# Ternary feed-forward inside the frequency attention, two batches behind it, and the first feed-forward's weights prepared in the first attention

## The reference

```python
# layer 0 feed-forward: bit-linear, depthwise convolution, silu, bit-linear
def weight_quant(w):
    scale = 1.0 / jnp.clip(jnp.mean(jnp.abs(w)), 1e-05)
    return jnp.clip(jnp.round(w * scale), -1, 1) / scale
def act_quant(x):                      # per position
    scale = 127.0 / jnp.clip(jnp.max(jnp.abs(x), axis=-1, keepdims=True), 1e-05)
    return jnp.clip(jnp.round(x * scale), -128, 127) / scale
# h = bit_linear(layernorm(x), w1); h = silu(conv3(h)); x += g * bit_linear(h, w2)
# w1 is 1024 x 256, w2 is 256 x 1024

# layer 1 attention (per batch): layernorm, rfft over the positions, 16 heads of
# attention of the 513 frequencies to those of the context, irfft, x += g * (y @ Wo.T)

# layer 1 feed-forward
delta = 0.7 * jnp.mean(jnp.abs(w))     # w is 256 x 256
wt = jnp.where(w > delta, 1.0, jnp.where(w < -delta, -1.0, 0.0))
# x += g * (alpha * layernorm(x) @ wt.T + bias)
```

## Time and profile before

| | |
|---|---|
| median of the runs | 1948.39 us (3 runs) |
| the profiled execution's own time | 1948.08 us |
| its span | 1946.1 us |
| TensorE busy | 1656.8 us (85% of the span) |
| DVE busy | 1148.0 us (59%) |
| ACT busy | 886.7 us (46%) |
| `l0x` from its first operation to its last | until 179.29 us |
| `l0f`, first operation to first `up` product | 180.67 to 213.58 us |
| `l1x` | 475.85 to 751.70 us |
| `l1f` | 752.93 to 806.24 us |

### The profile page before, as it was taken

One profiled execution on the slowest core, in us unless ns is written; L12 is line 12 of the kernel. 1 busy time (PEld: TensorE's weight loads), 2 busy tenths in 40 slices (PEclk: granted clock), 3 DMA queues, 4 the chain that ended last, 5 costly groups with the idle time before them and its releaser, 6 DMA issues. The chain is left out here.

```text
span 1946.1 us, 29978 instructions
## 1 busy us (share of the span) xinstructions
PE 1656.8 (85%) x10149; PEld 1254.6 (64%) x10149; DVE 1148.0 (59%) x2495; ACT 886.7 (46%) x1803; POOL 321.2 (17%) x359
## 2 busy tenths in 40 slices
PE   7895578896899997899997579999954999979998
PEld 5452245555677665588886269999944888854446
DVE  4765567676455556899887743322247889842115
ACT  2232567764443210365564345555544566533213
POOL 0000000000000001311100155555553111101110
PEclk9898799998899988999998779999977999979999
DMA  5001000002100000100001922222252000010002
GB/s 154 1 1 44 0 1 1 1 1 68 49 1 1 1 1 9 30 1 1 2 2 55 382 82 72 72 72 72 72 168 67 2 1 2 1 47 1 1 0 87
DMA packets 62845, 78.78 MB, mean 40 GB/s; under 512 B 13179, under 2 KB 52655, under 8 KB 62319
## 3 DMA queue, kind: packets, MB, share of 16 engines
q1 hardware_dynamic: 42967, 47.35, 7.4%
q0 software_dynamic: 7584, 20.72, 3.4%
q10 hardware_dynamic: 12152, 8.85, 1.5%
HBM read 58.16 MB, written 18.74 MB: 40 GB/s over the span
## 5 line engine op out<-in xcount | busy, mean ns | idle before, releaser
L2880 PEld LDWEIGHTS moe_bank<-moe_xt,moe_w1e 128*128 128x128 f32 x1264 | 155.0, 193 | 5.7 <-DVE moe_xt L2728 1.7
L2880 PE MATMUL moe_bank<-moe_xt,moe_w1e 128*128 128x128 f32 x1264 | 155.8, 277 | 1.1 <-DVE moe_xt L2728 1.1
L2890 PE MATMUL moe_bank<-moe_w,moe_xin 128*128 x632 | 149.3, 379 | 0.0
L2954 ACT ACTIVATE moe_xin<-moe_bank,moe_b 128x128 f32<-128x128 f32 x316 | 90.1, 368 | 125.8 <-PE moe_bank L2880 124.2
L390 PE MATMUL l0f_hb<-l0f_xt,l0f_w 128*128 128x512 f32 x256 | 126.0, 624 | 5.4 <-DVE l0f_a L321 3.8
L1092 POOL TENSOR_TENSOR all_x<-all_x,l1f_bias 128x256 f32 x32 | 23.1, 724 | 632.2 <-DVE l1f_xn L204 632.2
L2890 PEld LDWEIGHTS moe_bank<-moe_w,moe_xin 128*128 128x128 f32 x632 | 114.0, 190 | 12.3
L209 DVE BATCH_NORM_STATS2 all_stats<-all_x 128x6 f32<-128x256 f32 (+1 forms) x256 | 104.0, 422 | 8.4
L2737 DVE TENSOR_TENSOR moe_y<-moe_bank,moe_b2r 128x256 f32<-128x256 f32 x79 | 33.6, 425 | 119.0 <-PE moe_bank L2890 116.1
L2797 POOL DMA_INDIRECT moe_results<-moe_y,moe_row x79 | 78.0, 987 | 125.1 <-DVE moe_y L2737 121.1
L2728 DVE COPY moe_xt<-moe_bank 128x256 f32<-128x256 f32 x79 | 33.6, 425 | 106.2 <-PE moe_bank L2868 105.1
(11 more groups left out here) (478 smaller groups left out, 3812.1 us busy)
## 6 DMA issues: line engine op xcount, KB each, us to landing
moe_w<-in_L_ffn_W SPq DMA_DIRECT2D x32, 512.0 KB, 10.3
moe_w<-moe_results SPq DMA_DIRECT2D x16, 512.0 KB, 8.8
all_x<-in_x SPq DMA_DIRECT2D x4, 1024.0 KB, 13.1
out_x<-all_x SPq DMA_DIRECT2D x8, 512.0 KB, 2.9
l0f_w<-in_L_ffn_w_T SPq DMA_DIRECT2D x2, 1024.0 KB, 6.4
moe_inputs<-moe_xin ACTq DMA_DIRECT2D x8, 256.0 KB, 7.3
moe_inputs<-moe_w1e ACTq DMA_DIRECT2D x8, 256.0 KB, 7.5
moe_b2r<-in_L_ffn_b SPq DMA_DIRECT2D x1, 2048.0 KB, 14.0
```

The source lines that it names most:

```text
L2880: ins = nc.tensor.matmul(out, w1e[:, at:at + P], xt[:, u, c * P:(c + 1) * P], start=(c == 0), stop=(c == DC - 1))
L2890: ins = nc.tensor.matmul(bank[4 + u][:, 0:D], ht[:, u, c * P:(c + 1) * P], w2[:, ds(e * (HC * D) + c * D, D)], start=(c == 0), stop=(c == ...
L2954: ins = nc.scalar.activation(ht[:, u, m * P:(m + 1) * P], bank[1 + u][:, m * P:(m + 1) * P], ACT.Gelu, bias=b1[:, ds(e * HC + m, 1)])
```

## The change

1. A scope `f0` (w1, w2, scales, eight normalised tiles) lives over `l0x` and `l0f`. SP fetches `w1` and `w2` in `l0x`, behind the loads of `x`. In `l0x` ACT takes the two absolute sums at the end of round b=0, TensorE adds them over the partitions in round b=1, DVE makes the scales and rounds `w1` at the ends of rounds b=1 and b=2, and in round b=3 it computes the norm of the first eight tiles (`norm_range`), normalises them and makes their scales. `l0f` then starts with the eight quantising passes on ACT; the silu table and the scaling of `w2` come behind the first copies, the norm of the other 24 tiles behind the eight dequantising passes.
2. The stage `l1f` is gone. Its weights are fetched in `l1x`; DVE sums and rounds them in rounds b=0 and b=1. In rounds b=2 and b=3 the eight tiles of batch b-2 pass through the feed-forward in between the attention's work. Each takes one of the three `gbank` banks from its turn to its update, so `ORDER` gets 32 more names. Between a batch's last `update` and the `offset` of the next batch's query stands `next_norm` (the norm scale and shift of that batch, 19 small DVE operations). Behind the loop come the inverse and output of batch 3 with the feed-forward of batch 2 in between, then `next_norm(3)` and the feed-forward of batch 3 alone.
3. In rounds 1 to 3, `output(6)` of batch b-1 comes behind `scores(b, 4)` and ahead of `dft(b+1, 2)`; before it stood ahead of `values(b, 3)`.

```diff
 # l0x, ACT, end of round b
+                    if b == 0:
+                        act.wait_ge(sh.f0_loaded, 32)
+                        nc.scalar.activation(f.w2q[:, :, :].rearrange("p m d -> p (m d)"), f.w1[:, :, :].rearrange("p m d -> p (m d)"), ACT.Abs,
+                                             accum_out=f.wsum[:, 0:1]).then_inc(sh.f0_wsum, 1)
...
 # l0x, DVE, in round b
+                    else:
+                        dve.wait_ge(s.xn_ready, T)
+                        dve.wait_ge(s.stats_ready, 2 * TB)
+                        norm_range(nc, c, sh, 0, TB)
                     if b:
                         update(b - 1, 2)
                     if b + 1 < B:
                         norm(b + 1, NP, TB)
+                    else:
+                        next_inputs()
                     if b:
                         update(b - 1, 3)
+                        if b == 1:
+                            weight_scales()
+                        elif b == 2:
+                            round_weights()
+                        else:
+                            next_scales()
...
 # l0f, ACT
                 for t in range(TB):
-                    norm(t)
-                for t in range(TB):
                     quantise_x(t)
                 for t in range(0, TB, 2):
                     copy_x(t)
...
 # l1x, ORDER of rounds 1 to 3
+            ORDER += some("q2", b, 0, 4) + (some("sum", 0, 0) if b == 1 else ffn(0))
+            ORDER += some("it", b - 1, 0, 2) + ffn(1) + some("it", b - 1, 2, 4) + ffn(2)
+            ORDER += (some("dft", b + 1, 0, 2) if new else []) + ffn(3)
+            ORDER += some("out", b - 1, 0, 2) + ffn(4) + some("out", b - 1, 2, 5) + ffn(5) + some("out", b - 1, 5, 7) + ffn(6)
+            ORDER += (some("dft", b + 1, 2) if new else []) + some("out", b - 1, 7) + ffn(7)
...
 # l1x, DVE
+                def ffn_update(e, j):
+                    n = e * TB + j
+                    dve.wait_ge(s.fy_ps, n + 1)
+                    dve.wait_ge(s.f_biased, n + 1)
+                    nc.vector.tensor_tensor(x_tile(sh, n), gb("ffn", e, j)[:, D:2 * D], x_tile(sh, n), ALU.add).then_inc(s.fx_ready, 1)
...
                     if old:
                         update(b - 1, 6)
+                    if fed:
+                        ffn_update(e, 6)
+                    if old:
                         update(b - 1, 7)
+                    if fed:
+                        ffn_update(e, 7)
+                    if old:
+                        next_norm(b - 1)
+                    else:
+                        weight_sums()
                     if new:
                         offset(b + 1, 0)
                         offset(b + 1, 1)
...
 # l1x, PE
+                def ffn_turn(e, j):
+                    n = e * TB + j
+                    bank = free("ffn", e, j)
+                    pe.wait_ge(s.fxn_ready, n + 1)
```

More of the change, by code:

```diff
@@ L568, in stage_l0_xattn @@
     s = scope(nc, "l0x")
+    f = sh.f0
+    HID = 4 * D
     SC = D ** -0.5
@@ L1013, in _ @@
                         base(3)
+                    if b == 1:
+                        pe.wait_ge(sh.f0_wsum, 2)
+                        pe.wait_ge(s.shared_set, 1)
+                        nc.tensor.matmul(ub[:, 0:2], sh.ones[:, :], f.wsum[:, :], start=True, stop=True).then_inc(sh.f0_wtot, 1)
                     if b + 1 < B:
@@ L1246, in stage_l1_xattn @@
+        ORDER += some("it", B - 1, 0, 2) + some("ffn", B - 2, 0) + some("it", B - 1, 2, 4) + some("ffn", B - 2, 1)
+        for j in range(0, TB, 2):
+            ORDER += some("out", B - 1, j, j + 2) + some("ffn", B - 2, 2 + j // 2)
+        ORDER += some("ffn", B - 2, 6, 8) + some("ffn", B - 1, 0, 8)
         PLACE = {g: i for i, g in enumerate(ORDER)}
@@ L1397, in _, with weight_sums @@
                 offset(0, 1)
[L1398 to L1410 removed]
+                def weight_sums():
+                    dve.wait_ge(s.f_loaded, 48)
+                    nc.vector.tensor_reduce(fsum[:, :], fw[:, :, :], AX.XY, ALU.add, apply_absolute_value=True).then_inc(s.fsum_ready, 1)
@@ new lines, in _ @@
+                for b in range(B):
+                    old, new, e = b > 0, b + 1 < B, b - 2
+                    fed = e >= 0
+                    if old:
+                        result(b - 1, 4)
+                    if fed:
+                        ffn_norm(e, 0)
+                        ffn_norm(e, 1)
+                    shift(b, 0)
+                    if new:
+                        fold_halves(b + 1)
+                    sums(b, 0)
+                    if fed:
+                        ffn_update(e, 0)
+                    if b == 1:
+                        ternary_weights()
+                    result(b, 0)
+                    shift(b, 1)
@@ L1604, in _, with weight_total @@
                 pe.wait_ge(s.kbd_ready, 4)
-                for b in range(B + 1):
-                    live, old, new = b < B, b > 0, b + 1 < B
-                    if live:
-                        scores(b, 0)
-                        if b == 0:
-                            turn_values(0)
-                        for i in range(4):
-                            query(b, 1, i)
-                        turn(b, 0)
+                def weight_total():
+                    pe.wait_ge(s.fsum_ready, 1)
+                    nc.tensor.matmul(free("sum", 0, 0)[:, 0:1], sh.ones[:, :], fsum[:, :], start=True, stop=True).then_inc(s.fsum_ps, 1)
@@ L1614, in _ @@
+                for b in range(B):
+                    old, new, e = b > 0, b + 1 < B, b - 2
+                    fed = e >= 0
+                    scores(b, 0)
+                    if b == 0:
+                        turn_values(0)
+                    for i in range(4):
+                        query(b, 1, i)
+                    if b == 1:
+                        weight_total()
+                    if fed:
+                        ffn_turn(e, 0)
+                    turn(b, 0)
                     if old:
@@ L1636, in _ @@
+                    turn(b, 2)
                     if b == 0:
@@ L1673, in _ @@
                         dft(b + 1, 3)
+                    if fed:
+                        ffn_product(e, 7)
+                    if old and new:
                         dft(b + 1, 4)
                         dft(b + 1, 5)
-                    if live:
-                        values(b, 4)
+                    values(b, 4)
                     if new:
@@ L1680, in _ @@
                             query(b + 1, 0, i)
+                b, e = B - 1, B - 2
+                inverse(b, 0)
+                inverse(b, 1)
+                ffn_turn(e, 0)
+                inverse(b, 2)
+                ffn_product(e, 0)
+                inverse(b, 3)
+                ffn_turn(e, 1)
+                for j in range(0, TB, 2):
+                    output(b, j)
+                    ffn_product(e, 1 + j // 2)
+                    output(b, j + 1)
+                    ffn_turn(e, 2 + j // 2)
+                ffn_product(e, 5)
+                ffn_turn(e, 6)
+                ffn_product(e, 6)
+                ffn_turn(e, 7)
+                ffn_product(e, 7)
+                ffn_turn(b, 0)
+                for j in range(TB):
+                    if j + 1 < TB:
+                        ffn_turn(b, j + 1)
+                    ffn_product(b, j)
             @block.scalar
@@ L1809, in _ @@
                             copy_q(b + 1, 0, i)
+                for e in (B - 2, B - 1):
+                    for j in range(TB):
+                        ffn_copy(e, j)
 def stage_l3_ffn(nc, io, sh, out):
```

494 lines of the change are left out of this document (266 added, 228 removed).

## The result

The changed kernel takes 1918.31 us, the median of four runs (1916.69 to 1921.12), against 1948.36 us for the kernel before in the same comparison: a ratio of 0.985, 95% interval 0.9833 to 0.9867. The forecast was 1924, its range 1908 to 1945. The profiled execution took 1919.29 us, with a span of 1917.6.

The account below looks back on a forecast made before the run. The prediction took preparation waits to bound the start of `l0f`, and TensorE the loop of `l1x`. 1948.1 - 16.2 (part 1) - 8.5 (part 2) = 1923.4 us, 1923.7 against the median, stated as 1924; range 1908 to 1945, the forecast's own 1917 to 1931.

Parts of the forecast that it names:

- Part 1, the new beginning of `l0f`: Start of `l0f`: quantising passes 3.3 us, then 6.3 from first copy to first `up` product; a gain of 23.2 us.
- Part 1, what it adds in `l0x`: In `l0x`: absolute sums 3.9, clock dip 2.0, ones product 0.5, norm work left over 0.65; 7.0 us added.
- one more dip: In `l0x`, TensorE's clock falls after idling about 3.5 us behind ACT's sums, so products run slowly: 2.0 us.
- Part 2, the rounds: Loop of `l1x`: rounds 1, 2 and 3 change by -1.8, +13.3 and +10.1 us, +21.6 in all.
- for the late DVE: `l1x` round 2, before the next query: 1.5 us because two updates and statistics in front make DVE late.
- Part 2, the end: Behind the loop of `l1x`: from the inverse of batch 3 onward 50.6 us instead of 80.7, a gain of 30.1.
- rival B: `l1x` loop swallows the tiles in idle times: loops +13 instead of +21.6, 1915 us, or 1911 with `l0x` catching up; chance 0.20.
- A: In `l1x`, every feed-forward turn waits for a bank, clock dips each round: about 12 us more, 1936; chance 0.30 with D.
- C: In `l1x`, one chain of three banks makes each tile pay a full wait: loops cost 57 us, 1959 total; chance 0.09.
- D: Only part 1 gains, its `l0x` delay caught up or not; part 2 nets zero: 1932 us; chance 0.30 with A.
- GpSimd beside DVE: POOL's bias adds, 0.72 us a tile beside DVE in `l1x`, cost nothing; by the port-lock rule up to 17 us.
- The case that the prediction feared: In `l1x`, 24 GpSimd adds of 0.72 us lock out DVE's sums and folds, holding DVE for up to 17 us.

Follow-up runs that it names:

- the tiles behind the loop: Against the changed kernel, all 32 feed-forward tiles put behind the loop of `l1x`, `output(6)` left behind `scores(b,4)`: 1913.81 us.
- part 2 alone: Against the kernel before, only the second layer's feed-forward put inside `l1x`, with the first layer of before: 1936.14 us, ratio 0.9953.
- three updates early: Against the changed kernel, update 4, the feed-forward's update 5 and update 5 moved on DVE ahead of `result(b,3)` in rounds 1 to 3: 1910.67 us.

## Why the prediction was right

- **Part 1, the new beginning of `l0f`: right.** Forecast 9.6 us from the stage's first operation to the first `up` product and a gain of 23.2, measured 9.4 and 23.5.
- **Part 1, what it adds in `l0x`: mis-sized.** Forecast 3.9 + 2.0 + 0.5 + 0.65 = 7.0. Measured 2.1 in the exps' stretch (six profiles), 3.7 in one and 5.1 in two, and 0.2 to 0.3 for the rest in round 3. In the changed kernel's own profile it is 5.3. The step that failed is "DVE has no other work to bring forward, so I count 3.9 in full" together with one more dip: DVE's update was late by 3.2 us, but the wait of 3.58 us that stood later in the round, and its dip, shrank in return. The second dip came in three of nine executions, in which the two products there took 1.72, 1.76 and 2.05 us. I had cited that wait as the model for the new one and did not ask what became of it.
- **Part 2, the rounds: right in detail.** Forecast -1.8, +13.3, +10.1; measured -2.1, +12.9, +9.8 (+8.1 for round 3 in the executions at 54.4). Within round 2 the starts of `scores(2, 0)`, `(2, 3)`, `(2, 4)` and `(3, 0)` give +3.6, +4.1 and +5.2 for the forecast 3.5, 4.3 and 5.5. TensorE's waits were 0.79 and 0.87 where I had taken 1.1 twice, 2.47 where I had taken the same, and 1.88 where I had taken 1.8. The further 1.5 us "for the late DVE" have no wait of their own. The sum credits the third edit in round 1 alone; the tiles behind the loop show that it was worth 2.3 and 3.4 us in rounds 2 and 3 as well, and that the tiles used this up.
- **Part 2, the end: a little too good.** Forecast 50.6 from the inverse of batch 3 to the last statistics, measured 52.3 (724.58 to 776.84). The inverses took 16.8 as forecast; outputs with batch 2 17.6 for 16.8; the norm 3.6 as forecast; batch 3 14.3 for 13.4. Each of the last three tiles of batch 2 took 1.82 us (753.37, 755.20, 757.02), with a wait of 0.47 us for ACT's copy, where I had taken 1.6; why batch 3 took longer is not shown.
- **The total: in part luck.** Between the forecast (1923.4) and the profiled time (1919.29) lie 4.1 us. The terms of the sum miss by 1.3 together: 1.7 us less were added in `l0x` and 1.0 less in the rounds, 0.3 more were gained at the beginning, and 1.7 less were gained at the end. Then 3.3 us come from `l0f` behind its first product (2.1) and from the way to `scores(0, 0)` (1.2). The sum has no term for them, and kernels with the same code in these stages also differ by as much. The other stretches take 0.5 back. The median alone, 1918.31, lies nearer to rival B's 1915 than to 1924; it is the rounds that speak for the forecast.
- **The rivals.** A and C need a wait at every turn of the feed-forward; of the eight turns of round 2 one waits, 0.79 us. (C's sum leaves out round 1's -1.8 and would be 1957.) B is refuted by the tiles behind the loop. D is refuted by part 2 alone. Of the Trainium skill's rule on PSUM cycling ("TensorE: Matmul & The Clock Gate", "A second HAM failure mode: psum-queue depth-cycling") the trace shows a small piece at most: the clock in the last third of round 2 is 0.93, and 1.00 with three updates early, but it was already 0.91 there before the change (660.6 to 679.3 us).
- **GpSimd beside DVE: put at nothing, and nearly so.** The prediction says that the old stage shows nothing of a lock. It shows one case, and so does the changed kernel's end:

```profile
763.06 1.51 POOL L1472 TENSOR_TENSOR all_x<-all_x,l1x_fbias 128x256 f32<-128x256 f32 x2 [6.51 <-DVE l1x_fxn L204]
763.83 0.89 DVE L204 TENSOR_SCALAR l1x_fxn<-all_x,all_rstd,all_shift 128x256 f32<-128x256 f32 x1 [0.52 <-PE l1x_gbank L1631]
```

A normalise that takes 0.40 us elsewhere takes 0.89 beside two of GpSimd's adds back to back, and ends just behind the second (764.57); in the old stage one took 0.97 at 762.38. Eleven of the fourteen profiles have one such operation, of 0.89 to 0.98 us. Normalises that an add overlapped by 0.25 us or less kept 0.41, and additions from PSUM (0.42), statistics (0.43) and updates (0.48) kept their lengths beside adds. The Trainium skill ("SBUF — State Buffer", "SBUF: two separate sides") names for this lock also DVE operations in a two-port mode, which the prediction left out. The row fits a wait for a whole add; whether the normalise ran in such a mode no view shows. The case that the prediction feared is not tested: none of the sums of the forward transform (L1227, L1232) falls beside an add.

What part 2's gain consists of, by the tiles behind the loop: 7.8 us are the third edit's, 5.5 come from doing without the stage `l1f` with its barrier, its preparation and its start, and some 6 are lost again because half of the tiles in the loop stand where they cost most.

## What to carry to other kernels

Work that moves into a loop in which the bounding engine is full costs its own time there; whether the loop or its end is the better place has to be tried, as here, by putting the work behind the loop. When one change holds several edits, run each by itself: here the smallest, one output moved into a gap, gave more than the merging of two stages. Where buffers are handed out in a ring, find the release that comes late, and then the next two in the ring: moving one release gained nothing, moving three gained 3 us in round 2. A delay that is put ahead of a wait pays for itself in part; before adding it to the sum, look at what waits behind it.
